# Slot weights' last 64 rows on every second partition, with tokens' sums doubled and masked per partition

## The reference, cut to what matters

```python
logits = einsum('sd,btd->bst', sl, tok)
dispatch_w = softmax(logits, axis=-1)     # over tokens
combine_w = softmax(logits, axis=-2)      # over slots
y = einsum('btd,bst->bsd', xn, dispatch_w)
y = gelu(einsum('sio,bsi->bso', fc1_weight, y) + fc1_bias)
y = einsum('sio,bsi->bso', fc2_weight, y) + fc2_bias
out = einsum('bsd,bst->btd', y, combine_w)
```

## Time and profile before

| what | value |
|---|---|
| three runs | 1708.83, 1700.53, 1713.04 us |
| span of the profiled execution, first to last instruction | 1698.1 us |
| PE busy | 1444.5 us (85%) |
| DVE, ACT, POOL busy | 683.9, 662.5, 384.9 us |
| mean granted clock of TensorE | 0.900 |
| bytes moved by DMA | 178.73 MB, mean 105 GB/s |

### The profile page before, as it was taken

One profiled execution on the slowest core, in us unless ns is written; L12 is line 12 of the kernel. 1 busy time (PEld: TensorE's weight loads), 2 busy tenths in 40 slices (PEclk: granted clock), 3 DMA queues, 4 the chain that ended last, 5 costly groups with the idle time before them and its releaser, 6 DMA issues.

```text
span 1698.1 us, 31669 instructions
## 1 busy us (share of the span) xinstructions
PE 1444.5 (85%) x10300; PEld 1049.9 (62%) x10300; DVE 683.9 (40%) x2124; ACT 662.5 (39%) x2237; POOL 384.9 (23%) x464
## 2 busy tenths in 40 slices
PE   5899986796756778888899899699999999989994
PEld 3666664632212345666678799466765776789994
DVE  5557766511101376444423622433542423551113
ACT  1667663410000233777842122153663632213331
POOL 5212222300000122222200266220220200123441
PEclk8899996587778688999998899799999999889997
DMA  8434341679998400000003366200000200126553
GB/s 219 133 83 129 82 115 28 227 242 333 311 314 249 147 1 1 1 0 0 0 0 100 107 203 197 81 1 1 0 0 0 93 37 0 30 84 199 181 175 103
DMA packets 94439, 178.73 MB, mean 105 GB/s; under 512 B 35578, under 2 KB 54168, under 8 KB 92704
## 3 DMA queue, kind: packets, MB, share of 16 engines
q1 hardware_dynamic: 80144, 130.65, 26.1%
q10 hardware_dynamic: 7056, 30.67, 5.6%
q0 software_dynamic: 7136, 16.10, 3.1%
HBM read 150.39 MB, written 26.99 MB: 104 GB/s over the span
## 4 chain that ended last, share of the span: by engine, by line
PE 58%; issue 12%; DVE 12%; DMA 8%; ACT 6%; SPq 3%; POOL 1%; DVEq 0%; ACTq 0%; POOLq 0%
PE bank L1819 15%; DMA WM<-in_fc 7%; PE bank L2339 6%; PE bank L2325 4%; PE bank L1910 4%; PE bank L1922 3%; PE bank L1939 3%; PE bank L2329 3%; PE bank L1949 3%; PE bank L2000 2%; PE bank L1885 2%; PE bank L1992 2%; ACT ON L1604 2%; SPq L226 2%; PE bank L2256 1%
## 5 line engine op out<-in xcount | busy, mean ns | idle before, releaser
L1819 PE MATMUL bank<-XT,AREA 96*128 96x408 f32 (+1 forms) x640 | 239.1, 532 | 33.9 <-ACT XT L1558 16.6
L1819 PEld LDWEIGHTS bank<-XT,AREA 96*128 96x128 f32 (+1 forms) x640 | 122.1, 196 | 139.8 <-issue 99.8
L1910 PE MATMUL bank<-KZ,QT 128*102 128x102 f32 x1152 | 140.8, 262 | 9.0 <-ACT PB L1604 5.7
L664 POOL TENSOR_TENSOR PB<-PB,RCU 102x306 f32<-102x306 f32 x96 | 69.2, 720 | 318.5 <-DVE RCU L923 318.4
L648 POOL TENSOR_TENSOR RS<-VE,expo 102x4 f32<-102x4 f32 (+1 forms) x53 | 53.0, 1001 | 387.2 <-DVE VE L863 329.8
L1910 PEld LDWEIGHTS bank<-KZ,QT 128*102 128x102 f32 x1152 | 122.4, 174 | 27.2 <-issue 18.1
L2339 PE MATMUL bank<-WM,KZ 128*128 x660 | 118.2, 327 | 0.0
L2339 PEld LDWEIGHTS bank<-WM,KZ 128*128 128x128 f32 x660 | 105.7, 190 | 0.4
L1585 ACT ACTIVATE KZ<-bank,AREA 128x128 f32<-128x128 f32 x198 | 54.6, 374 | 121.8 <-PE bank L2329 121.8
L1922 PE MATMUL bank<-AREA,OT 128*102 128x192 f32 x384 | 88.9, 345 | 11.3 <-DVE SLOTS L1276 5.3
L1939 PE MATMUL bank<-PT,V 102*32 102x102 f32 (+1 forms) x1152 | 85.9, 270 | 14.5 <-DVE OT L933 12.3
(11 more groups left out here) (335 smaller groups left out, 2777.5 us busy)
## 6 DMA issues: line engine op xcount, KB each, us to landing
AREA<-in_fc SPq DMA_DIRECT2D x10, 1536.0 KB, 26.1
SLOTS<-in_m3w SPq DMA_DIRECT2D x33, 384.0 KB
WM<-in_fc ACTq DMA_DIRECT2D x5, 2304.0 KB, 19.5
WM<-in_fc SPq DMA_DIRECT2D x6, 1536.0 KB, 27.9
AREA<-in_fc ACTq DMA_DIRECT2D x4, 2304.0 KB, 20.6
SLOTS<-in_m1w SPq DMA_DIRECT2D x33, 256.0 KB
AREA<-pos_scratch SPq DMA_DIRECT2D x16, 459.0 KB
pos_scratch<-AREA SPq DMA_DIRECT2D x8, 913.5 KB
```

Of the source, the lines that this page charges most:

```text
L664: pool.tensor_tensor(p, p, scale, ALU.mult).then_inc(sem["probs_ready"], 1)
L1819: last = pe.matmul(dst, lhsT, rhs, start=n == 0, stop=n == len(pieces) - 1)
L1910: last = pe.matmul(psum[k][0:T, cols(j)], QT[:, tile, cols(bb)], KALL[:, unit % per_tile * (HEADS // per_tile) + tile, cols(bb)], start=Tr ...
```

## The change

The two half loads now write each row of 768 numbers to every second partition: the even slots' rows 128 to 191 to partitions 0, 2, ... 126, the odd slots' to 1, 3, ... 127. Feature 128 + i of an even slot then lies on partition 2i, of an odd slot on 2i + 1. To meet it, YTH gets a full set of 64 slots on 128 partitions, in which feature 128 + i stands on partitions 2i and 2i + 1, and is zero on the partitions of the other parity; `into_slots` multiplies over all 128 partitions.

YTH is made so: POOL copies the last 64 features of each group into XD with every feature twice in a row (`twice`); PE sums the tokens with XD as weights of 128 columns, which replaces line 2111 and now stands ahead of line 2107; ACT copies the result in two pieces, even and odd slots, each scaled by a column that is 1 on partitions of its parity and 0 on the others. DVE makes these two columns (`parity`) from the identity at the start. There are two buffers of XD, with a semaphore each way. The buffer SLOTS has room for the larger YTH. Nothing else is changed.

```diff
-YTC = 3 * NSLOT // 2 * NB + 2 * NB
+YTC = 2 * NSLOT * NB + 2 * NB
...
-                engine.dma_start(HALF[j][64 * odd:64 * odd + 64], rows[128:D, odd:RING:2]
+                engine.dma_start(HALF[j][odd:128:2], rows[128:D, odd:RING:2]
...
+            def twice(g):
+
+                pool.wait_ge(sem["xn_ready"], NG + 2 + g)
+                if g >= 2:
+                    pool.wait_ge(sem["xd_used"], g - 1)
+                src = XND[g][:, :, 128:D].unsqueeze(3).to_broadcast([T, GB, 64, 2])
+                pool.tensor_copy(XD[g % 2][:].rearrange("p b (d o) -> p b d o", o=2), src
+                                 ).then_inc(sem["xd_ready"], 1)
...
-            for buf, n in ((YTF, NSLOT), (YTH, NSLOT // 2)):
-                pool.memset(buf[:, n * NB:(n + 1) * NB], 0.0).then_inc(sem["yt_padded"], 1)
+            for buf in (YTF, YTH):
+                pool.memset(buf[:, NSLOT * NB:(NSLOT + 1) * NB], 0.0).then_inc(sem["yt_padded"], 1)
+            twice(0)
             for g in range(NG):
                 if g + 1 < NG:
                     power(0)
+                    twice(g + 1)
                     power(1)
                 dispatch(g)
...
+            for odd in range(2):
+                dve.tensor_reduce(parity[:, odd:odd + 1], ident[:, odd:128:2], AX.X, ALU.add
+                                  ).then_inc(sem["parity_ready"], 1)
...
+            act.wait_ge(sem["parity_ready"], 2)
             turned(XT)
...
-                free(activation(YTS[1][:, :, g * GB:(g + 1) * GB], src[1], ACT.Copy), k)
+                for odd in range(2):
+                    last = activation(YTS[1][:, odd:NSLOT:2, g * GB:(g + 1) * GB], src[1][:, odd:NSLOT:2, :],
+                                      ACT.Identity, bias=0.0, scale=parity[:, odd:odd + 1])
+                free(last, k)
...
+                pe.wait_ge(sem["xd_ready"], g + 1)
+                for bb in range(GB):
+                    c = GB * NSLOT + bb * NSLOT
+                    last = pe.matmul(p[:, c:c + NSLOT], XD[g % 2][:, bb, :], DW[g % 2][:, bb, :], start=True, stop=True)
+                last.then_inc(sem["xd_used"], 1)
                 for bb in range(GB):
                     c = bb * NSLOT
-                    pe.matmul(p[:, c:c + NSLOT], x[:, bb, 0:128], DW[g % 2][:, bb, :], start=True, stop=True)
-                for bb in range(GB):
-                    c = GB * NSLOT + bb * NSLOT // 2
-                    for odd in range(2):
-                        last = pe.matmul(p[64 * odd:64 * odd + 64, c:c + NSLOT // 2], x[:, bb, 128:D],
-                                         DW[g % 2][:, bb, odd:NSLOT:2], start=True, stop=True)
+                    last = pe.matmul(p[:, c:c + NSLOT], x[:, bb, 0:128], DW[g % 2][:, bb, :], start=True, stop=True)
...
-                        s, rows = RING * q + r, slice(64 * (r % 2), 64 * (r % 2) + 64)
-                        pe.matmul(o[32 * r:32 * r + 32], YTH[rows, NB * (s // 2):NB * (s // 2) + 32],
-                                  HALF[j][rows, r // 2, c0:c1], start=False, stop=False)
+                        s = RING * q + r
+                        pe.matmul(o[32 * r:32 * r + 32], YTH[:, NB * s:NB * s + 32],
+                                  HALF[j][:, r // 2, c0:c1], start=False, stop=False)
```

More of the change, by code:

```diff
@@ L183, in build @@
         YTF, YTH = SLOTS[:, 0:NSLOT * NB + NB], SLOTS[:, NSLOT * NB + NB:YTC]
-        YTS = [buf[:, 0:n * NB].rearrange("p (s b) -> p s b", s=n) for buf, n in ((YTF, NSLOT), (YTH, NSLOT // 2))]
+        YTS = [buf[:, 0:NSLOT * NB].rearrange("p (s b) -> p s b", s=NSLOT) for buf in (YTF, YTH)]
         BIAS, PICK = V[0:NSLOT, 0:FF], V[0:NSLOT, FF:FF + 32 * NSLOT]
@@ L270, in build @@
         ones = sb("ones", [128, 128])
+        parity = sb("parity", [128, 2])
+        XD = [sb(f"XD{j}", [T, GB, 128]) for j in range(2)]
         marked = sb("marked", [1, 8])
@@ L403, in build @@
                "conv_ready", "gate_ready", "gated",
-               "combine_in", "dispatch_in", "yt_padded",
+               "combine_in", "dispatch_in", "yt_padded", "parity_ready", "xd_ready", "xd_used",
                "bias_loaded", *(f"{w}_{x}{j}" for w in ("fc1", "fc2") for x in ("loaded", "used") for j in range(QRING)),
@@ L1705, in _ @@
                 there = full(k)
-                src = [there[:, c:c + GB * n].rearrange("p (b s) -> p s b", b=GB)
-                       for c, n in ((0, NSLOT), (GB * NSLOT, NSLOT // 2))]
+                src = [there[:, c:c + GB * NSLOT].rearrange("p (b s) -> p s b", b=GB) for c in (0, GB * NSLOT)]
                 activation(YTS[0][:, :, g * GB:(g + 1) * GB], src[0], ACT.Copy)
-                free(activation(YTS[1][:, :, g * GB:(g + 1) * GB], src[1], ACT.Copy), k)
+                for odd in range(2):
+                    last = activation(YTS[1][:, odd:NSLOT:2, g * GB:(g + 1) * GB], src[1][:, odd:NSLOT:2, :],
+                                      ACT.Identity, bias=0.0, scale=parity[:, odd:odd + 1])
+                free(last, k)
             at.first_banks()
```

## The result

| comparison | changed, median of runs | before, median of runs | ratio, 95% interval |
|---|---|---|---|
| first | 1651.3 us (1649.3 to 1663.8, 4 runs) | 1704.7 us (4) | 0.9706 [0.9667, 0.9745] |
| second | 1663.3 us (1656.5 to 1667.2, 4 runs) | 1705.5 us (7) | 0.9743 [0.9692, 0.9794] |
| third | 1661.3 us (1644.4 to 1664.6, 6 runs) | 1699.7 us (11) | 0.9735 [0.9680, 0.9790] |

The forecast was 1677 us in a range of 1664 to 1718: right in its direction, and 26 us above the first result, which lies under the range. The median of all 14 runs of the changed kernel is 1661.3. The ratios leave out six runs in a slower state: four of the 19 of the kernel before that ran beside e1 to e4 (the median of its other 15 is 1697.5 us), one of e2, and one of f3 (2098.5 us at a granted clock of 0.628).

What follows compares the result with a forecast made beforehand. The prediction took the slot stage to be bound by its DMA transfers. From the profiled 1698.1 us, minus 37 for loads, plus 4.9 for dispatch gave 1666; plus 10.7 to the runs' median gave 1677 us, range 1664 to 1718.

Steps and rivals of the forecast that it cites:

- The bound: Slot stage: it lasts as long as its transfers, 61.4 MB in 194.4 us at 316 GB/s, slowed beside the 64-partition half loads.
- the signs: Changed profile: slices 10 to 12 at 370 GB/s or more, no dips, half loads 1.0 us apart, stage over at about 530.
- the rate given to the half loads: Slot stage refills: half loads and second weights beside them at 361 GB/s, 12.1 us a quad, 37 us less over 13.
- 96-partition load: Analogue for the strided half loads: 271 GB/s on the mean against 311 for three quarters of 415, so 0.87 kept.
- the upper bound: Slot stage: half loads run like the others, 61.3 MB at 415 GB/s in 148 us, 46 us less.
- The level: Whole kernel: the median of the runs, 1708.8 us, lies 10.7 us above the profiled span, so 10.7 was added.
- The dispatch: Token sums on the chain, four times: PE products +0.9 us (+3.7 in all), ACT copies +0.3 us (+1.2), together +4.9.
- POOL's copy: Dispatch, doubling copy of 512 elements, four times: about 0.5 to 0.6 us each, hidden, 0; without cover 2.4 us.
- Second matmuls: Slot stage: eight with 128 rows take 1.93 us like eight with 64 rows, so 0.
- Half the gain: Rival, slot stage: engines meet in pairs in the same partitions' path; stage 18 us shorter, kernel 1696 us; chance 0.22.
- no gain: Rival, slot stage: slow stretches come from something else in the loads; only the costs stay, 1714 us; chance 0.17.
- The slower case: Rival, slot stage: strided loads hold up everybody, second weights too; +13 us and the 4.9, 1727 us; chance 0.13.

Runs made afterwards that it cites:

- e1: Kernel before with only the half loads sent to every second partition, sums unchanged (second halves of products wrong): 1653.6 us, ratio 0.9738.
- e4: Kernel before with the last 64 rows of first weights laid out ahead, one 128-partition load per quad replacing two half loads: 1652.8 us, ratio 0.9753.
- e2: Changed kernel with its half loads back on 64 adjacent partitions, doubled and masked sums kept (products wrong): 1697.9 us, ratio 1.0025.
- f3: Changed kernel with each half load cut in four of 16 rows, each to every eighth partition over all 128: 1693.3 us, ratio 0.9928.
- e5: Changed kernel with each half load cut in two of 32 rows, each to every fourth partition over all 128: 1661.6 us, ratio 0.9749.
- f1: Changed kernel with one half load per refilled quad instead of two, on partitions 0 to 63 (products wrong): 1674.5 us, ratio 0.9835.
- f2: Changed kernel with one half load per refilled quad instead of two, on partitions 32 to 95 (products wrong): 1652.0 us, ratio 0.9672.
- e8: Changed kernel with the 1536 KB load of each quad cut in two of 64 adjacent partitions: 1727.2 us, ratio 1.0119.

## Why the prediction was right in sign and wrong in size

**The bound.** Right. Half loads on 64 partitions held the line under its speed, the line bound the stage, and the gain appeared where it was placed: slices 10 to 12 at 417 and more (370 was asked), no dips, less waiting. Three of the signs came out otherwise: the half loads of quad 1 land 1.7 us apart and not 1.0, the first long piece of the chain is 27.0 us and not under 25, and the stage ended at 510.7 us and not at 530. The long pieces were taken for waits; TensorE itself waited 8.7 us at most.

**The step that failed: the rate given to the half loads (361 GB/s, minus 37 us).** It was read off a 96-partition load that kept 0.87 of "its share". The half loads run at 415 to 418, and so do the loads beside them. Ten profiles with the loads at full rate (changed three times, loads alone, packed, and packed and doubled twice each, e5 once) have stages of 164.7 to 176.6 us, mean 170.6: 46 us less than the 216.8 of before, which is the upper bound that the prediction had named (148 us of transfers, minus 46). The 216.8 is one profile; e2, with the same slow loads, has 220.1. The analogue was a wrong one: by the rule of f1 to f3, partitions 0 to 95 put 64 rows on one side and 32 on the other, and that gives the three quarters, 311 GB/s, but not the 271 of the earlier trace rows. The factor that was carried over is the step from 311 to 271; its reason is open, and the strided half loads do not show it.

**The level, 6 us.** The sum was lifted by 10.7 us to the median of three runs, 1708.8. The five comparisons had medians of 1697.5 to 1706.7 for the same kernel, mean 1702.8.

**The draw, 10 us.** The first four runs have a median of 1651.3, all 14 have 1661.3. Two things vary from execution to execution, and TensorE's granted clock goes with both. Whether the chip adds to it is not told apart: the comparisons were not all on one. First, the slot stage began at 340 to 345 us in eleven of the 18 profiles, at 348 to 355 in the other seven. The stretch from 150 to 200 us in the changed kernel and then in f2, whose stage began at 351.7 us:

```profile
150.00:200.00 50.00, 45.52 (x356) 31.16 (x355) 33.97 (x90) 35.17 (x134) 11.06 (x16) 0.97 0.40 110
```

```profile
150.00:200.00 50.00, 46.20 (x318) 30.68 (x318) 30.02 (x80) 29.39 (x109) 8.69 (x12) 0.83 0.29 80
```

Granted 0.83 in place of 0.97, in code that neither kernel touched. Over 100 to 250 us the granted clock is 0.97 or 0.98 in all eleven early profiles and 0.91 to 0.94 in all seven late ones. Second, the stage itself: 7.85 us to the first refill if quad 0 meets a rising clock (first profile) and 9.9 if not (second); and a quad that starts at the low clock takes 13.4 us in place of 7.6, so it matters whether one of the last quads does. In the changed kernel's first profile the last two quads ran at the full clock, in the second the last one started at the low clock, after TensorE had waited 5.1 us for its load: 165.6 against 176.6. The spans follow: 1647.5 + 7.5 (later start) + 11.0 (longer stage) = 1666.0, and the second profile's is 1665.5. Of the first pair's 51.2 us between stages, 5 were this draw. Why the clock falls in one execution and not in another was not tried.

**The dispatch, +4.9.** +4.1 on the chain (four times 0.70 for the products and 0.35 for the copies, less 0.1). The products were forecast at 0.9 and are 0.70, because the second group adds 1.72 behind the first and not 1.97; the copies were forecast at 0.3 and are 0.35. POOL's copy at 0.61 and the mask at 0.35 are hidden, as said.

**Second matmuls, 0.** Slightly wrong: 7.64 us for 7.90 per quad. Quads wait for loads most of the time, so it is worth 2 us at most, an estimate.

Added up: 1677 - 9 (load term) - 1 (dispatch) - 6 (level) = 1661, the median of all runs, and the draw makes the first result 1651. That the first result was 10 us below the median is luck, not mechanism.

**The rivals.** Half the gain and no gain are out by e1. (In the first, 0.9 us by 13 quads are 12 us, not 13.) The slower case is out too: the second weights are not held up by strided loads, as both queues together hold 418 GB/s.

**The range** was too narrow at its low end: it stopped at the upper bound of one term (by the prediction's own numbers 1698.1 - 46 + 4.9 + 10.7 = 1668, not 1665) and left no room for the spread of the runs, which was in sight (1700.5 to 1713.0 before).

## What to carry to other kernels

When a stage is bound by its transfers, read GB/s in slices of a microsecond and look for the loads that stand beside each dip; ask of each load not how many partitions it has but whether it meets, on both sides of partition 64, all eight places that a group of four has in a block of 32. Every second partition, or rows packed ahead for 128, gave the half loads here the rate of full ones. Here a bound worked out from the best rows of the same kernel was a better value than an analogue whose own reason is unknown. The range has to add the spread of the runs to that of the terms.

## What the runs showed that was not expected

The line from HBM held 417 GB/s over 140.4 us, not only for the bursts of before; full slices of the pages at the full rate read 416 to 420. The Trainium skill, "DMA: Bandwidth & Descriptors", section "Where 436 GB/s comes from", has loads from HBM bound at about 358 for a core; these rows, with one core at work, disagree, and the measurement decides.

Products with 128 rows were a little shorter than those with 64 in the same place, behind products with 128 rows: each of a quad's two groups is 0.13 us shorter. The reason was not tried. TensorE's groups by form in one quad of the changed kernel, then of before:

```profile
L2150 PE MATMUL bank<-KZ,SLOTS 128*32 128x512 f32 x8 | 1.0, 592 | 0.0
L2150 PE MATMUL bank<-KZ,SLOTS 128*32 128x256 f32 x8 | 0.6, 379 | 0.0
```

```profile
L2132 PE MATMUL bank<-KZ,SLOTS 64*32 64x512 f32 x8 | 1.1, 601 | 0.0
L2132 PE MATMUL bank<-KZ,SLOTS 64*32 64x256 f32 x8 | 0.6, 388 | 0.0
```

Loads that reach half of the groups cost more than their own bytes. Alone on the line they ran at about 220 GB/s instead of 415, 2.1 us more per MB. In the stage, over 13 refills, 0.39 MB of them a quad cost 24.5 us (f1 against f2), 0.79 MB cost 46 (before against the ten), 1.57 MB cost 70 (e8 against the ten): 4.8, 4.5 and 3.4 us per MB. The other queue's loads are slowed beside them, which is likely the rest; it was not measured apart, and each of these kernels has one profile.
